# Order of work around the turned gates in a gated-delta-rule layer between two FFNs

## The chip, the core and the metric

The kernel runs on one core of a Trainium2 chip. The time is the device time of one execution in microseconds; the median of three runs of the kernel before is 4090.89 us. Engines work side by side, each through a queue of its own in program order: TensorE (PE), VectorE (DVE), ScalarE (ACT), GpSimd (POOL) and SyncE (SP), which here only issues DMAs. They wait for each other on semaphores.

## The reference

```python
x = x + 0.5 * ffn(layernorm(x))      # spline-built weights
x = x + attn(layernorm(x))
x = x + 0.5 * ffn(layernorm(x))

# attn, for 4 sequences of 512 tokens, 16 key heads of width 128, 2 value heads each
qkvz = x @ W_qkvz                    # q, k, v, z per key head
q, k, v = silu(causal_conv4(q, k, v))
q = rms_norm(q) / D;  k = rms_norm(k) / sqrt(D)
beta = sigmoid(b);    g = -exp(A_log) * softplus(a + dt_bias)
def step(S, q_t, k_t, v_t, g_t, beta_t):       # for every token
    S = S * exp(g_t)
    delta = (v_t - k_t @ S) * beta_t
    S = S + outer(k_t, delta)
    return S, q_t @ S
out = silu(z) * (rms_norm(o) * norm_w)
return out @ W_out
```

## The kernel before

A first FFN runs to about 430 us, the second from about 3790 us. Between them `attn_phase` works through 64 units: a unit is one sequence of 512 tokens of one key head with its two value heads (called head 0 and 1 here), in four chunks of 128 tokens. The recurrence inside a chunk is a triangular system; its 128x128 matrix is inverted in 7 levels of doubling for each head. With the two heads in turn this makes the steps 0 to 13 (`s`; head `s % 2`, level `s // 2`). A step from 2 on is a loop through four engines: TensorE makes a product into the bank `psP` (`at_prod`), VectorE masks it into fp16 (`at_pm`, line 2053), TensorE adds 8 small products into the head's inverse (`psT[g]`, `at_inv`, lines 1675 and 1677), and ScalarE copies that to fp16 (`at_t`, line 1869; `copy_t`). Level 0 (`level_0`, line 1607) seeds the inverse of a head; ScalarE copies it whole (line 1867). Its result for head 0 and 1 of unit j+1 is made at the end of the slot of unit j.

The passes `pe_pass`, `act_pass`, `dve_pass` and `pool_pass` each write out one engine's queue for slots j = -1 to 63. A slot holds the inverse of unit j, its four chunks of recurrence (behind step 15), the preparation of unit j+1 (projections `proj_part`, convolution `tap` and `conv`, `silu`, norms, decays), and the output of unit j-1. The order is written by hand. On TensorE, step s is: product, then the tasks in `fill[s]`, then the inverse products; what is in `fill[s]` hides the mask. `gap[...]` are the tasks between the parts of the chunks. On ScalarE and VectorE the tasks of `steps[s]` stand behind the copy or mask of step s.

The fills are made of these:
- `proj_part(u, first, end)`: products `first` to `end` of 12, 512 columns each, of a projection of unit j+1 (Q, K, V0, V1). `gates_in(u, first, end)`: products of 24, 256 columns each, of Z0 or Z1 of unit j. K, V0 and Z0 share a bank, Q, V1 and Z1 the other; `bank_free` waits for the last reader (for Z0 the last tap of K's convolution).
- `turn_gated(h, j-1)` (line 1528): transposes the gated output of head h of the unit before into the bank `psM` (`at_misc`). It waits for POOL's scaling (`scale_gated`, line 2155) and, for head 1, for VectorE's low half of head 0. ScalarE takes the high half from the bank (`gated`, line 1883, `at_gt_hi`), VectorE the low half (`low`, line 2020, `at_gt_lo`).
- `out_product(c, j-1)`: 6 products with the two halves into the same bank; VectorE adds them to the residual (`out_add`, line 2026) before the next.
- `turn_k`, `turn_kn`, `sums`, `gram_of`, `decay`, `kq_of`: for the norm of k, its product with itself, the decays and q k.

VectorE's `qk(h)` (line 2001) multiplies q k by the decays of head h; its end also releases SP's load of the next weights. At the end of a slot ScalarE squares the outputs (`squares`, line 1877), head 1 first; VectorE multiplies them by the gates of z (line 2094). The output of head 1 lies in `psP`, that of head 0 in `psT[1]`. POOL makes the scales, and in every fourth unit splits the next weights into high and low (lines 2126, 2127), the Z part in two halves, the first when `s_z` tells that Z1's last product is done.

Of the kernel before, what the change touches and what calls it, by code (L numbers as in the profile page):

```python
# [28 lines left out]
ACT = mybir.ActivationFunctionType  # L29
# [5 lines left out]
NK, NV, R = 16, 32, 2  # L35
# [1217 lines left out]
K_U, Q_U, V0_U, V1_U, Z0_U, Z1_U = range(6)  # L1253
# [8 lines left out]
def attn_phase(nc, w_qkvz, conv_w, norm_w, w_out, cst_in, cst16_in, resid, x_hi, x_lo, gate_dram, decay_dram, y_dram):  # L1262
# [7 lines left out]
    with ExitStack() as ctx:  # L1270
# [101 lines left out]
        def wait(eng, name, value):  # L1372

            value += AHEAD.get(name, 0)
            if value > 0:
                eng.wait_ge(sems[name], value)
# [81 lines left out]
        def pe_pass(pe):  # L1458
# [5 lines left out]
            for j, has_delta, has_prep, behind, ends in slots():  # L1464
# [18 lines left out]
                def proj_part(u, first, end, i=j):  # L1483

                    if first == 0:
                        unit = i if u >= Z0_U else i + 1
                        if unit % B == 0:
                            if u >= Z0_U:
                                wait(pe, "p_z", unit // B + 1)
                            else:  # L1490
                                wait(pe, "p_w", 2 * (unit // B) + (1 if u in (K_U, Q_U) else 2))
                        bank_free(u, i)
                    tok = (i if u >= Z0_U else i + 1) % B * S
                    for k in range(first, end):
                        hb = k // 3
                        w, xs = ((w_hi, x_hi), (w_hi, x_lo), (w_lo, x_hi))[k % 3]
                        last = mm(unit_bank[u][:], w[:, hb, UNIT_COL[u]:UNIT_COL[u] + D], xs[:, hb, tok:tok + S], k == 0, k == 3 * HB - 1)
                    if end == 3 * HB:
                        own["s_z" if u >= Z0_U else "s_proj"].up(last)
# [110 lines left out]
                def parts(u, first, end, i=j):  # L1610
                    return lambda: proj_part(u, first, end, i)
# [3 lines left out]
                def gates_in(u, first, end):  # L1615
                    return lambda: gate_part(u, first, end)

                if has_prep:
                    fill[2].append(parts(Q_U, 8, 12))
                if has_delta:  # L1620
                    fill[3].append(gates_in(Z0_U, 0, 6))
                    fill[4].append(gates_in(Z0_U, 6, 16))
                    fill[5].append(gates_in(Z0_U, 16, 20))
                    fill[6].append(gates_in(Z0_U, 20, 24))
                    fill[7].append(gates_in(Z1_U, 0, 10))
                    for s in range(3):
                        fill[9 + s].append(gates_in(Z1_U, 10 + 3 * s, 13 + 3 * s))
                if behind:
                    for h in range(R):
                        fill[5 + h].append(lambda h=h: turn_gated(h, j - 1))  # L1630
                    for c in range(WPROD):
                        fill[8 + c].append(lambda c=c: out_product(c, j - 1))
                if has_delta:
                    fill[12].append(gates_in(Z1_U, 19, 24))
                if has_prep:
                    fill[12].append(turn_k)
                    fill[13].append(parts(V0_U, 0, 3))
                    fill[14].append(parts(V0_U, 3, 6))
                    fill[15] += [parts(V0_U, 6, 9), sums]
                    gap[0].append(parts(V0_U, 9, 12))  # L1640
                    gap[1].append(lambda: gram_of(j + 1))
                    gap[2].append(lambda: decay(0))
                    gap[3].append(parts(V1_U, 0, 4))
                    gap[4] += [lambda: decay(1), parts(V1_U, 4, 5)]
                    gap[5].append(parts(V1_U, 5, 9))
                    gap[6].append(parts(V1_U, 9, 12))
                    gap[10] += [lambda: level_0(j + 1, 0), lambda: kq_of(j + 1)]
                    if j + 2 < UNITS:
                        gap[6].append(parts(K_U, 0, 1, j + 1))
                        gap[7].append(parts(K_U, 1, 5, j + 1))  # L1650
                        gap[8].append(parts(K_U, 5, 7, j + 1))
                        gap[9].append(parts(K_U, 7, 12, j + 1))

                if not has_delta:
                    proj(K_U, range(HB))
                    proj_part(Q_U, 0, 8)
                for s in range(R, STEPS):
                    g, level = s % R, s // R
                    if has_delta:

                        if level == 1:
                            wait(pe, "a_hi", R * j + g + 1)
                            wait(pe, "a_sqo", R * j)
                            wait(pe, "d_gate", R * j)
                        wait(pe, "a_t", STEPS * j + s - R + 1)
                        for c in range(CH):
                            last = mm(ch(psP, c), ch(nlhi[:, g], c), ch(t16[:, g, 0], c))
                        own["s_p"].up(last)
                    for task in fill[s]:
                        task()  # L1670
                    if has_delta:

                        wait(pe, "d_p", PSTEPS * j + s - R + 1)
                        for c in range(CH):
                            nc.tensor.matmul(half_of(ch(psT[g], c), level, 0), ch(t16[:, g, 1], c), half_of(ch(pm[:, g], c), level, 0),  # L1675
                                             start=False, stop=True, skip_group_check=True)
                            last = nc.tensor.matmul(half_of(ch(psT[g], CH + c), level, 1), ch(pm[:, g], c),  # L1677
                                                    half_of(ch(t16[:, g, 1], c), level, 1),
                                                    start=False, stop=True, skip_group_check=True)
                        own["s_t"].up(last)  # L1680
# [83 lines left out]
                        task()  # L1764
                if has_prep:
                    if j + 2 < UNITS:
                        proj_part(Q_U, 0, 8, j + 1)
                    level_0(j + 1, 1)
                if ends:
                    for h in range(R):  # L1770
                        turn_gated(h, j)
# [5 lines left out]
        def act_pass(act):  # L1777
            own = counters("a_")
            A = nc.scalar.activation
            for j, has_delta, has_prep, behind, ends in slots():  # L1780
                nxt = (j + 1) % 2
                kh, gcur, at = j // B, *gates_of(j)

                def conv_out(u):
                    return (cv_k[:], cv_q[:], cv_v[:, nxt, 0, :], cv_v[:, nxt, 1, :])[u]

                def tap(u, j=j):

                    wait(act, "s_proj", 4 * j + u + 1)
                    if u == Q_U and has_delta:  # L1790
                        wait(act, "s_kq", j + 1)
                        wait(act, "p_qg", R * (j + 1))
                    if u == V0_U:
                        wait(act, "s_o", j)
                    own["a_tap"].up(A(conv_out(u), unit_bank[u][:], ACT.Copy, scale=cw[(j + 1) // B % 2][:, u, 3:4]))  # L1795

                def tanh(u):

                    if u == K_U:
                        wait(act, "d_silu", j)  # L1800
                    elif u == Q_U:
                        wait(act, "p_silu", 3 * j)
                    elif has_delta:
                        wait(act, "d_z", 2 * j + u - 1)
                    else:
                        wait(act, "p_silu", 3 * j + u - 1)
                    wait(act, "d_conv", 4 * j + u + 1)
                    own["a_th"].up(A(th[:, u % 2, :], conv_out(u), ACT.Tanh, scale=0.5))

                def tanh_z(u):  # L1810
                    if has_prep:
# [73 lines left out]
                steps = {s: [] for s in range(R, STEPS + 1)}  # L1885
                if has_prep and not has_delta:
                    steps[2].append(lambda: tap(K_U))
                if has_prep:
                    steps[2].append(lambda: tap(Q_U))
                    steps[3].append(lambda: tanh(K_U))  # L1890
                if behind:
                    for h in range(R):
                        steps[5 + h].append(lambda h=h: gated(j - 1, h))
                if has_prep:
                    steps[7].append(lambda: tanh(Q_U))
                if has_delta:
# [52 lines left out]
                        squares(h)  # L1949
                if has_prep:  # L1950
                    copy_t(j + 1, 1)
                    tanh(V1_U)
                if ends:
                    for h in range(R):
                        gated(j, h)
# [2 lines left out]
        def dve_pass(dve):  # L1958
# [8 lines left out]
            for j, has_delta, has_prep, behind, ends in slots():  # L1967
# [61 lines left out]
                if has_prep and has_delta:  # L2029
                    steps[2].append(lambda: conv(K_U, (3,)))  # L2030
                if has_delta:
                    steps[2].append(lambda: qk(0))
                    steps[3].append(lambda: qk(1))
                if has_prep:
                    if not has_delta:
                        steps[3].append(lambda: conv(K_U, (1, 2, 3)))
                if has_prep:
                    steps[3].append(lambda: conv(Q_U, (1,)))
                    steps[4].append(lambda: conv(Q_U, (2, 3)))
                if behind:  # L2040
                    for h in range(R):
                        steps[5 + h].append(lambda h=h: low(h, j - 1))
                    for c in range(WPROD):
                        steps[8 + c].append(lambda c=c: out_add(c, j - 1))
                if has_delta:
# [346 lines left out]
```

How the kernel before makes its waits and increments, by code:

```python
            @block.gpsimd  # L380
            def _(pool):
                nc.gpsimd.memset(f32(st_g[:]), 0.0).then_inc(zeroed, 1)
                nc.gpsimd.memset(f32(st_b[:]), 0.0).then_inc(zeroed, 1)
                pool.dma_start(wts[:, 0:2 * GSUM], gsum_in).then_inc(sums_in, 16)
                pool.dma_start(groups(wts, S_FD, 4 * P), dsum_in.rearrange("p (g n) -> p g n", g=4)).then_inc(sums_in, 16)
                for u in range(UNITS + 4):
                    pool.wait_ge(hi_done, u + 1)
                    nc.gpsimd.tensor_tensor(weights(u, False), quarters(merged[:, u % 2, :]), f32(weights(u, True)), ALU.subtract).then_inc(lo_done, 1)
                pool.wait_ge(lo_done, UNITS + 4)
                pool.wait_ge(sums_in, 32)
# [1 line left out]
            @block.vector  # L392
# [4 lines left out]
                def chain(ins):  # L397
                    count[0] += 1
                    ins.then_inc(link, 1)
                    dve.wait_ge(link, count[0])
# [24 lines left out]
                    V.tensor_scalar(d3, c3, 0.5 * step ** 3, None, ALU.mult)  # L425
                    chain(V.tensor_scalar(d1, c1, 0.5 * step, None, ALU.mult))
                    if reach:
                        chain(V.scalar_tensor_tensor(d1, d3, float(reach), d1, ALU.mult, ALU.add))
                dve.wait_ge(tap_g_in, 32)
                cubics(tap_g, phi_g, d_g, NG, 0)
                dve.wait_ge(zeroed, 1)
# [30 lines left out]
                for u in range(UNITS + 4):  # L463
                    if u == 0:
                        dve.wait_ge(eval_in, 32)
                    if u == UNITS:
```

## Time and profile before

| | |
|---|---|
| median of 3 runs | 4090.89 us (4090.2 to 4093.23) |
| profiled execution | 4097.49 us, its span 4095.7 us |
| mean granted TensorE clock | 0.973 |
| PE busy | 3670.1 us, 90% |
| PE weight loads busy | 3033.4 us, 74% |
| POOL busy | 2327.9 us, 57% |
| DVE busy | 2314.6 us, 57% |
| ACT busy | 2058.3 us, 50% |

The busy time of PE includes the tail of each pipelined matmul, so neighbours overlap: the distance between two starts is what a product costs in a full stream. A row of the timeline has the start, the duration, engine, line, operation, output<-inputs, shapes and count, and in brackets the idle time of the engine ahead of it and the instruction whose end released it. Most of TensorE's products have line 1462, that of a helper.

### The profile page before, as it was taken

How to read it: one execution, taken by the hardware profiler on the slowest of the kernel's cores; microseconds unless marked ns; L12 is line 12 of the kernel's file. 1: busy time of each engine (PE TensorE's matmuls, PEld its weight loads, DVE VectorE, ACT ScalarE, POOL GpSimd, SP SyncE). 2: the span in 40 equal slices, each digit the busy share in tenths (PEclk: the TensorE clock that was granted, in tenths of full speed). 3: DMA queues.
4: the chain of work that ended last, by engine and by line, in shares of the span. 5: the costliest groups of instructions: out<-in, count | busy, mean ns of one | idle time of the engine just before them, and what ended most of it. 6: DMA issues, size and time to landing. Idle time of an engine off the chain costs nothing. (4 is left out here: it accounts for less than half of the span.)

```text
span 4095.7 us, 76858 instructions
## 1 busy us (share of the span) xinstructions
PE 3670.1 (90%) x29348; PEld 3033.4 (74%) x29348; DVE 2314.6 (57%) x4155; ACT 2058.3 (50%) x5168; POOL 2327.9 (57%) x2899
## 2 busy tenths in 40 slices
PE   5995699999999999999999999999999999997798
PEld 4884577777777777777777777777777777776587
DVE  4554455555555555555555555555555555554464
ACT  3442355555555555555555555555555555554233
POOL 2111567676767676666666666666666676763111
PEclk8997899999999999999999999999999999998799
DMA  4332100000000000000000000000000000001421
GB/s 175 81 42 55 54 17 28 17 28 17 28 17 28 17 23 22 23 22 23 22 23 22 23 22 23 22 23 22 23 22 19 21 22 22 22 17 37 171 52 32
DMA packets 142395, 140.46 MB, mean 34 GB/s; under 512 B 84176, under 2 KB 115152, under 8 KB 140880
## 3 DMA queue, kind: packets, MB, share of 16 engines
q1 hardware_dynamic: 136992, 120.16, 10.4%
q0 software_dynamic: 4464, 14.36, 0.9%
q8 instruction: 236, 3.87, 0.4%
q14 instruction: 127, 1.04, 0.1%
q10 hardware_dynamic: 576, 1.03, 0.1%
HBM read 109.11 MB, written 26.21 MB: 33 GB/s over the span
## 5 line engine op out<-in xcount | busy, mean ns | idle before, releaser
L1869 ACT ACTIVATE at_t<-at_inv 128x512 f16<-128x512 f32 x768 | 459.2, 598 | 869.9 <-PE at_inv L1677 869.8
L2053 DVE TENSOR_TENSOR at_pm<-at_prod,at_cst 128x512 f16<-128x512 f32 x768 | 525.8, 685 | 103.4 <-PE at_prod L1462 101.2
L1462 PE MATMUL at_proj<-x_hi,at_w_hi 128*128 128x512 f32 x1024 | 443.9, 434 | 25.9 <-POOL at_w_lo L2127 16.1
L1462 PE MATMUL at_proj<-x_hi,at_w_lo 128*128 128x512 f32 x1024 | 421.8, 412 | 0.0
L1462 PE MATMUL at_proj<-x_lo,at_w_hi 128*128 128x512 f32 x1024 | 417.0, 407 | 0.0
L1675 PEld LDWEIGHTS at_inv<-at_pm,at_t 128*128 128x128 f16 x3072 | 202.7, 98 | 286.4 <-DVE at_pm L2053 206.4
L1675 PE MATMUL at_inv<-at_pm,at_t 128*128 128x64 f16 x3072 | 293.4, 196 | 114.9 <-DVE at_pm L2053 107.4
L1462 PE MATMUL at_prod<-at_t,at_nlhi 128*128 128x128 f16 x3584 | 370.7, 220 | 8.6 <-DVE at_pm L2060 0.9
L2212 POOL TENSOR_TENSOR at_gt_lo<-at_cst,at_gates 128x512 fp32r<-128x512 f32 x256 | 261.6, 1043 | 133.1 <-PE at_misc L1462 133.0
L2026 DVE TENSOR_TENSOR resid<-at_misc,resid 128x512 f32<-128x512 f32 x256 | 177.1, 692 | 278.4 <-PE at_misc L1462 278.4
L1462 PE MATMUL at_proj<-at_w_hi,x_lo 128*128 128x256 f32 x1024 | 319.6, 312 | 0.0
L1462 PE MATMUL at_proj<-at_w_hi,x_hi 128*128 128x256 f32 x1024 | 310.5, 303 | 2.6
L1462 PE MATMUL at_proj<-at_w_lo,x_hi 128*128 128x256 f32 x1024 | 296.4, 290 | 0.0
L1978 DVE SCALAR_TENSOR_TENSOR at_cv_v<-at_proj,at_cw,at_cv_v 128x511 f32<-128x511 f32 (+2 forms) x384 | 287.5, 749 | 15.5 <-ACT at_cv_v L1795 2.0
L1677 PE MATMUL at_inv<-at_t,at_pm 128*128 128x64 f16 x3072 | 286.7, 194 | 0.0
L1462 PEld LDWEIGHTS at_prod<-at_t,at_nlhi 128*128 128x128 f16 x3584 | 236.0, 98 | 34.4 <-issue 33.4
L889 PE MATMUL f_ring<-f_x_hi,ffn_w 128*128 128x512 f32 x640 | 247.8, 402 | 2.9 <-DVE f_x_lo L815 2.9
L1934 ACT ACTIVATE at_t<-at_inv,at_gates 128x128 f32<-128x128 f32 x512 | 160.1, 365 | 175.4 <-PE at_inv L1462 175.4
L1923 ACT ACTIVATE at_t<-at_inv 128x256 f32<-128x256 f32 x256 | 98.5, 385 | 290.9 <-PE at_inv L1734 277.0
L1462 PEld LDWEIGHTS at_proj<-x_hi,at_w_hi 128*128 128x128 f32 x1024 | 195.5, 191 | 54.8 <-issue 21.8
L1462 PE MATMUL at_misc<-at_wo_hi,at_gt_hi 128*128 128x512 f32 x512 | 230.3, 450 | 4.0 <-DVE resid L2026 2.4
L2020 DVE SCALAR_TENSOR_TENSOR at_gt_lo<-at_misc,at_nw,at_gt_hi 128x512 fp32r<-128x512 f32 x128 | 96.2, 751 | 228.2 <-ACT at_gt_hi L1883 228.2
(291 smaller groups left out, 10819.0 us busy)
## 6 DMA issues: line engine op xcount, KB each, us to landing
at_gb<-decays SPq DMA_DIRECT2D x64, 512.0 KB, 3.7
at_e<-w_qkvz SPq DMA_DIRECT2D x32, 512.0 KB, 3.7
ffn_weights<-ffn_w SPq DMA_DIRECT2D x1, 11776.0 KB, 36.5
ffn_w<-ffn_weights POOLq DMA_DIRECT2D x4, 2688.0 KB, 23.8
at_gb<-w_qkvz SPq DMA_DIRECT2D x16, 512.0 KB, 3.7
at_gb<-w_out SPq DMA_DIRECT2D x16, 512.0 KB, 3.5
f_xnext<-x_in SPq DMA_DIRECT2D x4, 1024.0 KB, 5.3
f_xres<-x_res SPq DMA_DIRECT2D x4, 1024.0 KB, 5.1
```

The costliest lines, as they stand in the source:

```text
L889: return nc.tensor.matmul(out, lhsT, rhs, start=start, stop=stop)
L1462: return nc.tensor.matmul(out, lhsT, rhs, start=start, stop=stop)
L1675: nc.tensor.matmul(half_of(ch(psT[g], c), level, 0), ch(t16[:, g, 1], c), half_of(ch(pm[:, g], c), level, 0), start=False, stop=True, skip ...
L1677: last = nc.tensor.matmul(half_of(ch(psT[g], CH + c), level, 1), ch(pm[:, g], c), half_of(ch(t16[:, g, 1], c), level, 1), start=False, sto ...
L1869: own["a_t"].up(A(grown(t16[:, s % R].rearrange("p a t -> p (a t)"), s // R), grown(psT[s % R], s // R), ACT.Copy))
L1923: own["a_v"].up(A(vp, psV, ACT.Copy))
L1934: own["a_d"].up(A(delta[:, h, :], ch(psY, h), ACT.Copy, scale=gcur[:, 2, at + c, h:h + 1]))
L1978: ins = V.scalar_tensor_tensor(out[:, s:S], unit_bank[u][:, 0:S - s], cw[(j + 1) // B % 2][:, u, 3 - s:4 - s], out[:, s:S], ALU.mult, ALU.add)
L2020: own["d_lo"].up(V.scalar_tensor_tensor(gt_lo[:, h, :], out_bank[:], nw[:, 0:1], gt_hi[:, h, :], ALU.mult, ALU.subtract))
L2026: own["d_y"].up(V.tensor_tensor(row, out_bank[:], row, ALU.add))
L2053: own["d_p"].up(V.tensor_tensor(pm[:, g].rearrange("p (c t) -> p c t", c=CH), psP[:].rearrange("p (c t) -> p c t", c=CH), mask.unsqueeze(1 ...
L2212: last = G.tensor_tensor(gm[:, k], incl.unsqueeze(1).to_broadcast([P, CH, P]), new_gates[:, g, at:at + CH, h:h + 1].to_broadcast([P, CH, P ...
```

## The change

Nothing is added or taken out of the computation; instructions change their places in three queues and two waits follow them.

- TensorE: `level_0(j, 1)` moves from the end of slot j-1 to step 2 of slot j, behind step 2's product and the last 3 Q products (before: 4; the ninth moves to the end of the slot before). Behind it stand the first 4 products of Z0, so Z0 starts a step earlier; Z1 is 8, 2, 2, 2, 5, 5 products in steps 7, 9, 10, 11, 12, 13 (before 10, 3, 3, 3, 5 to step 12). V0 starts in step 14 (before 13). The product of step 2 waits for the squares of head 1 only, that of step 3 for both.
- ScalarE: the high halves of heads 0 and 1 stand in steps 4 and 5, ahead of the copies of steps 5 and 6 (before: behind them). The tanh of V1 moves from the slot's end to step 2 of the next, Q's tap and K's tanh each a step later.
- VectorE: both `qk` stand behind the mask of step 3 (before: one in step 2). The Q convolution's taps 1 and 2 stand in step 4 (before: 1 in step 3, 2 and 3 in step 4), tap 3 in step 5 behind the low half of head 0.

```diff
                 if has_prep:
-                    fill[2].append(parts(Q_U, 8, 12))
+                    fill[2].append(parts(Q_U, 9, 12))
                 if has_delta:
-                    fill[3].append(gates_in(Z0_U, 0, 6))
-                    fill[4].append(gates_in(Z0_U, 6, 16))
-                    fill[5].append(gates_in(Z0_U, 16, 20))
-                    fill[6].append(gates_in(Z0_U, 20, 24))
-                    fill[7].append(gates_in(Z1_U, 0, 10))
+                    fill[2] += [lambda: level_0(j, 1), gates_in(Z0_U, 0, 4)]
+                    fill[3].append(gates_in(Z0_U, 4, 10))
+                    fill[4].append(gates_in(Z0_U, 10, 18))
+                    fill[5].append(gates_in(Z0_U, 18, 21))
+                    fill[6].append(gates_in(Z0_U, 21, 24))
+                    fill[7].append(gates_in(Z1_U, 0, 8))
                     for s in range(3):
-                        fill[9 + s].append(gates_in(Z1_U, 10 + 3 * s, 13 + 3 * s))
+                        fill[9 + s].append(gates_in(Z1_U, 8 + 2 * s, 10 + 2 * s))
...
                 if has_delta:
-                    fill[12].append(gates_in(Z1_U, 19, 24))
+                    fill[12].append(gates_in(Z1_U, 14, 19))
+                    fill[13].append(gates_in(Z1_U, 19, 24))
                 if has_prep:
                     fill[12].append(turn_k)
-                    fill[13].append(parts(V0_U, 0, 3))
-                    fill[14].append(parts(V0_U, 3, 6))
-                    fill[15] += [parts(V0_U, 6, 9), sums]
+                    fill[14].append(parts(V0_U, 0, 4))
+                    fill[15] += [parts(V0_U, 4, 9), sums]
...
-                            wait(pe, "a_sqo", R * j)
+                            wait(pe, "a_sqo", R * j - 1 + g)
                             wait(pe, "d_gate", R * j)
...
-                        proj_part(Q_U, 0, 8, j + 1)
-                    level_0(j + 1, 1)
+                        proj_part(Q_U, 0, 9, j + 1)
...
+                if has_delta:
+                    steps[2].append(lambda: tanh(V1_U, j - 1))
                 if has_prep:
-                    steps[2].append(lambda: tap(Q_U))
-                    steps[3].append(lambda: tanh(K_U))
+                    steps[3].append(lambda: tap(Q_U))
+                    steps[4].append(lambda: tanh(K_U))
                 if behind:
                     for h in range(R):
-                        steps[5 + h].append(lambda h=h: gated(j - 1, h))
+                        steps[4 + h].append(lambda h=h: gated(j - 1, h))
...
                     copy_t(j + 1, 1)
-                    tanh(V1_U)
...
                 if has_delta:
-                    steps[2].append(lambda: qk(0))
-                    steps[3].append(lambda: qk(1))
+                    steps[3] += [lambda: qk(0), lambda: qk(1)]
                 if has_prep:
                     if not has_delta:
                         steps[3].append(lambda: conv(K_U, (1, 2, 3)))
+                    steps[4].append(lambda: conv(Q_U, (1, 2)))
+                if behind:
+                    steps[5].append(lambda: low(0, j - 1))
                 if has_prep:
-                    steps[3].append(lambda: conv(Q_U, (1,)))
-                    steps[4].append(lambda: conv(Q_U, (2, 3)))
+                    steps[5].append(lambda: conv(Q_U, (3,)))
                 if behind:
-                    for h in range(R):
-                        steps[5 + h].append(lambda h=h: low(h, j - 1))
+                    steps[6].append(lambda: low(1, j - 1))
```

## Rows read from the trace of the kernel before

**Rows 1.** Busy time by engine in unit 30: length, busy (count), PEclk, DMA, GB/s

```profile
2021.89:2073.62 51.73, 47.62 (x419) 39.69 (x419) 30.27 (x55) 28.14 (x75) 34.57 (x43) 1.00 0.07 21
```

**Rows 2.** TensorE's timeline over the end of slot 29 and slot 30

```profile
2019.37 0.40 PE L1462 MATMUL at_proj<-x_lo,at_w_hi 128*128 128x512 f32 x1
2020.21 0.38 PE L1462 MATMUL at_inv<-at_pm,at_cst 128*128 128x512 f16 x1 [0.45 <-ACT at_aqk L1877]
...
2020.65 0.39 PE L1462 MATMUL at_prod<-at_t,at_nlhi 128*128 128x128 f16 x4
...
2022.76 0.28 PE L1462 MATMUL at_proj<-at_w_hi,x_lo 128*128 128x256 f32 x1
2022.87 0.28 PE L1462 MATMUL at_proj<-at_w_lo,x_hi 128*128 128x256 f32 x1
...
2023.74 0.20 PE L1675 MATMUL at_inv<-at_pm,at_t 128*128 128x64 f16 x1 [0.25 <-DVE at_pm L2053]
...
2026.72 0.60 PE L1528 MATMUL at_misc<-at_cst,at_cv_z 128*128 128x128 f32 x4
2027.76 0.20 PE L1675 MATMUL at_inv<-at_pm,at_t 128*128 128x64 f16 x1 [0.43 <-DVE at_pm L2053]
...
2030.32 0.63 PE L1528 MATMUL at_misc<-at_cst,at_cv_z 128*128 128x128 f32 x4 [1.40 <-DVE at_gt_lo L2020]
...
2033.89 0.20 PE L1675 MATMUL at_inv<-at_pm,at_t 128*128 128x64 f16 x1 [1.20 <-DVE at_pm L2053]
...
2050.53 0.66 PE L1568 MATMUL at_misc<-at_cst,at_kn 128*128 128x128 f32 x4
```

**Rows 3.** ScalarE's timeline in slot 30

```profile
2020.85 1.02 ACT L1867 ACTIVATE at_t<-at_inv 128x1024 f16<-128x1024 f32 x1 [0.73 <-PE at_inv L1607]
...
2024.19 0.60 ACT L1869 ACTIVATE at_t<-at_inv 128x512 f16<-128x512 f32 x1 [0.68 <-PE at_inv L1677]
...
2028.21 0.60 ACT L1869 ACTIVATE at_t<-at_inv 128x512 f16<-128x512 f32 x1 [1.44 <-PE at_inv L1677]
2028.70 0.68 ACT L1883 ACTIVATE at_gt_hi<-at_misc,at_nw 128x512 fp32r<-128x512 f32 x1
...
2049.34 1.14 ACT L1838 ACTIVATE at_kn<-at_misc,at_scale 128x128 f32<-128x128 f32 x4
```

**Rows 4.** VectorE's timeline in slot 30

```profile
2019.11 0.69 DVE L2094 TENSOR_TENSOR at_cv_z<-at_prod,at_cv_z 128x512 f32<-128x512 f32 x1 [0.41 <-ACT at_aqk L1877]
...
2021.14 0.69 DVE L2053 TENSOR_TENSOR at_pm<-at_prod,at_cst 128x512 f16<-128x512 f32 x1 [0.69 <-PE at_prod L1462]
...
2025.58 1.52 DVE L1978 SCALAR_TENSOR_TENSOR at_cv_q<-at_proj,at_cw,at_cv_q 128x510 f32<-128x510 f32 x2
...
2029.42 0.75 DVE L2020 SCALAR_TENSOR_TENSOR at_gt_lo<-at_misc,at_nw,at_gt_hi 128x512 fp32r<-128x512 f32 x1 [1.72 <-ACT at_gt_hi L1883]
...
2033.15 0.68 DVE L2053 TENSOR_TENSOR at_pm<-at_prod,at_cst 128x512 f16<-128x512 f32 x1
...
2038.44 0.69 DVE L2026 TENSOR_TENSOR resid<-at_misc,resid 128x512 f32<-128x512 f32 x1 [1.15 <-PE at_misc L1462]
```

**Rows 5.** POOL's timeline in slot 30, and in slot 31 (from 2096 us)

```profile
2022.83 2.04 POOL L2155 TENSOR_TENSOR at_cv_z<-at_cv_z,at_fr 128x512 f32<-128x512 f32 x2
...
2032.06 1.04 POOL L2126 CAST at_w_hi<-at_e 128x1024 fp32r<-128x1024 f32 x1
...
2096.29 0.61 POOL L2126 CAST at_w_hi<-at_gb 128x512 fp32r<-128x512 f32 x1 [2.58 <-PE at_proj L1462]
...
2098.64 0.23 POOL L2218 TENSOR_SCALAR at_rr<-at_ss 128x4 f32<-128x4 f32 x1 [0.38 <-issue]
```

**Rows 6.** Busy time by engine in a stretch of slot 24, columns as in rows 1

```profile
1719.00:1723.20 4.20, 3.98 (x29) 3.75 (x30) 1.84 (x3) 1.18 (x2) 4.20 (x5) 0.59 0.18 69
```

**Rows 7.** TensorE's timeline in slot 24, the second turned gate

```profile
1719.04 0.99 PE L1528 MATMUL at_misc<-at_cst,at_cv_z 128*128 128x128 f32 x4 [1.39 <-DVE at_gt_lo L2020]
```

**Rows 8.** DMA issues by tile: queue, count, KB each, us to landing

```profile
at_e<-w_qkvz SPq DMA_DIRECT2D x32, 512.0 KB, 3.7
```

More of the change, by code:

```diff
@@ L1655, in pe_pass @@
                     proj(K_U, range(HB))
-                    proj_part(Q_U, 0, 8)
+                    proj_part(Q_U, 0, 9)
                 for s in range(R, STEPS):
@@ L1782, in act_pass, with conv_out @@
                 kh, gcur, at = j // B, *gates_of(j)
-                def conv_out(u):
-                    return (cv_k[:], cv_q[:], cv_v[:, nxt, 0, :], cv_v[:, nxt, 1, :])[u]
+                def conv_out(u, i=j):
+                    return (cv_k[:], cv_q[:], cv_v[:, (i + 1) % 2, 0, :], cv_v[:, (i + 1) % 2, 1, :])[u]
                 def tap(u, j=j):
@@ L1795, in tap, with tanh @@
                     own["a_tap"].up(A(conv_out(u), unit_bank[u][:], ACT.Copy, scale=cw[(j + 1) // B % 2][:, u, 3:4]))
-                def tanh(u):
+                def tanh(u, i=j):
                     if u == K_U:
-                        wait(act, "d_silu", j)
+                        wait(act, "d_silu", i)
                     elif u == Q_U:
-                        wait(act, "p_silu", 3 * j)
-                    elif has_delta:
-                        wait(act, "d_z", 2 * j + u - 1)
-                    else:
-                        wait(act, "p_silu", 3 * j + u - 1)
-                    wait(act, "d_conv", 4 * j + u + 1)
-                    own["a_th"].up(A(th[:, u % 2, :], conv_out(u), ACT.Tanh, scale=0.5))
+                        wait(act, "p_silu", 3 * i)
+                    elif i >= 0:
+                        wait(act, "d_z", 2 * i + u - 1)
+                    else:
+                        wait(act, "p_silu", 3 * i + u - 1)
+                    wait(act, "d_conv", 4 * i + u + 1)
+                    own["a_th"].up(A(th[:, u % 2, :], conv_out(u, i), ACT.Tanh, scale=0.5))
                 def tanh_z(u):
```

## The prediction

> **What bounds the kernel now.** I read the busy times of one unit first [rows 1]: of its 51.73 us TensorE is busy in 47.62, at full clock, POOL, the next, in 34.57. 62 units in a row are within 0.6 us of this length. TensorE's queue sets the time, so only its waits and what it executes matter. What is executed doesn't change here; only the order does.
>
> Then I read TensorE's timeline of one unit (unit 30) for its stalls [rows 2]. The reader sees 0.45 us until the squares on ScalarE are done (2020.21), 0.25 and 0.43 us for a mask (2023.74, 2027.76), 1.40 us in front of the second turned gate (2030.32) and 1.20 us for the mask of step 7 (2033.89). The records' ends overlap the next start, so I count from where the stream could have gone on (last start plus pitch; pitches 0.117 us for a 256-column and 0.235 us for a 512-column product). Then the stalls are: squares 0.60, mask 2 0.10, mask 3 0.41, mask 4 0.27, mask 5 0.60, turned gate 1.56, mask 7 1.36, and six small ones behind step 8, 0.93 together: **5.8 us of 51.7**. Nothing larger than that can be won in a unit.
>
> The two largest have one cause. ScalarE takes the high half of a turned gate only after the inverse copy of the same step (2028.70 behind the copy at 2028.21), VectorE takes the low half from it (2029.42) and TensorE's next transpose into the same bank waits for that low half [rows 2 to 4]. The next mask stands behind the low half in VectorE's queue (2033.15).
>
> **Latencies used**, from rows 2 to 4: first product to its mask 0.45 us (2020.65 to 2021.14 is 0.49; I take a little less, as an estimate); mask start to inverse products 0.74 (2033.15 to 2033.89); first inverse product to ScalarE's copy 0.45 (2023.74 to 2024.19); VectorE's pitch 0.61 for a mask, 0.65 to 0.76 for a convolution tap; a fill of n gate products takes 0.09 + 0.117n behind the 0.20 us of the product ahead of it.
>
> **The change part by part**, on unit 30's clock, where the time at which Q's first products run is the same in both.
>
> *First product of step 2 ahead of level 0.* It no longer waits for the squares of head 0, but for the gate product that reads its bank (VectorE 2019.11 + 0.69) and for the ninth Q product (2019.84). It starts at 19.90, not 20.65. Mask 2 is at 20.4, the last K tap at 21.0 to 21.75. TensorE goes on with three Q products (0.79) and level 0 of head 1 from 20.88 (0.43), which is past the squares' end (20.12) by itself: **the 0.60 us stall is gone**. But now two things come late. The first Z product needs the bank of K, free with the last K tap, so it starts at 21.80 (stall 0.49). And ScalarE copies level 0's result at 21.52 instead of 20.85 [rows 3], 1.02 us long, so the product of step 3 can't start before 22.62. Inverse 2 runs at 22.40, 0.5 us later than now (21.89), with 4 gate products (0.47) more behind it: so far nothing is won.
>
> *Steps 3 and 4.* Product 3 at 22.64, mask 3 at 23.09, inverse 3 at 23.84; the two decay products now stand behind that mask (ends 24.9; they delayed mask 3 before), so mask 4 starts at 24.89 and inverse 4 at 25.64 (now 25.72), with 2 gate products more done. Q's tap is at 24.79 on ScalarE and tanh of K at 26.6; the convolution's first two taps follow mask 4 (25.5, 26.25), mask 5 is at 26.93, inverse 5 at 27.68 (now 27.76).
>
> *SP's queue.* The second decay product also releases the load of the next weights. It ends 0.7 us later (24.97), and 3.7 us to landing [rows 8] is before POOL reads them (2032.06, rows 5): nothing, with some 3 us to spare.
>
> *Turned gates.* The first one runs at 26.53. The POOL scaling it needs has ended by 24.9 [rows 5] (2022.83 + 2.04), so nothing new holds it. ScalarE's high half is at 27.18, straight behind it, not 28.70; the low half at 27.90 (now 29.42); the second turned gate at 28.80 (now 30.32; stall 0.23). Mask 6 stands behind the low half and the last Q tap (28.55 to 29.2): 29.20, and inverse 6 at 29.95 (now 30.83; stall 0.7). The second high half is at 29.46, its low half at 30.18, mask 7 at 30.84, inverse 7 at **31.59, now 33.89**. That is 2.30 us earlier, with 8 of Z1's products behind it where there are 10 now.
>
> *Steps 8 to 11.* The output products use one bank: last product, add on VectorE (2038.44, 0.69), next product. That chain makes a step 2.44 us long now, and with 2 gate products in place of 3 it stays 2.44. So the shorter fill wins nothing, and 5 gate products (0.59 us) are owed at step 12.
>
> *Steps 12 and 13 and behind.* Step 12 has the same work. Step 13 has 5 gate products in place of 3 V0 products; its inverse comes at 43.79, now 46.25 (2.46 earlier), owing 3 V0 products (0.70). One of these fills the 0.28 us that the second residual waits for now; the last Newton product is 1.97 us earlier, and the turning of the scaled k, which now waits for ScalarE's scaling (2049.34 + 1.14, then 2050.53), is 2.10 us earlier, since the scaling moved forward by 2.4. From there to the end of the unit every wait is triggered by TensorE's own products, so I carry 2.10 through. The ninth Q product at the unit's end was counted from the start. The tanh of V1 leaves ScalarE's queue behind level 0's copy and stands behind the next one (23.3): POOL needs it at 24.83, so it costs nothing; were it later than that, POOL would slip by the rest, which its idle time ahead of the k scale hides.
>
> *Every fourth unit.* POOL splits the next Z weights in two halves, the first when Z1's last product is done: 2096.29 in unit 31, followed by the scale of k at 2098.64 [rows 5]. Z1's last product moves from step 12 to step 13, so this start is only 0.76 us earlier. On unit 30's clock the scale's chain starts at 46.15 and takes 1.6; k is scaled at 47.85 to 49.0 and turned at 49.04, not 48.43: these units win 1.5 instead of 2.1.
>
> **Sum.** 47 units x 2.10 + 15 x 1.5 = 121, the first and last unit some 2 more: 123 us. The profiled execution took 4097.5 us (span 4095.7); by it 3974. The median is 4090.9, so **3968 us** (ratio 0.970).
>
> **The clock.** From 1719.0 to 1723.2 the granted clock averages 0.59 [rows 6]: it fell to the lower of its two levels (1.2 GHz) just after the 1.39 us stall and ran the turned gate in 0.99 instead of 0.63 us [rows 7]. Twelve of the 62 units show such a fall and are 0.2 to 0.5 us longer, 4 us in all. Unknown after the change: without the 1.4 us stall it may vanish (-4 us); or the stretch of 27.0 to 30.0, which has 1.6 us of stalls and two groups of transposes in 3 us, may bring it oftener. Taken at 0, as neither end is nearer. The Trainium skill ("TensorE: Matmul & The Clock Gate", Part 4: PE-mode transpose) says that transposes don't count as work for the clock gate in the way products do, which speaks against this change: by it the new stretch is the emptier one and (c) below the likelier, while by the row, in which the longest stall comes just before the fall, the new one is the fuller and the sum gains 4 us.
>
> **Rivals.**
> (a) *The masks take the place of the gate waits.* If the first high half comes later than I walk (its transpose stands behind mask 5's chain of two Q taps), low half, last Q tap and mask 6 pile up in VectorE's queue, which already holds 3.5 us of work between 26.9 and 30.8. Each slip of one 0.7 us instruction delays masks 6 and 7 both; with one slip in each the gain is 2.1 - 1.4 = 0.7 us a unit, 45 us: 4046. With half of that, 4007. For it: VectorE is without a pause in that stretch of my walk. Against: the high half waits for nothing but the transpose.
> (b) *The order doesn't act*: what the turned gates wait for is the scaled gate on POOL. Then about 4089. Against: rows 5, 1.6 us of room.
> (c) *Slower, by the clock.* Falls in every unit. The fall in rows 6 lasts (1 - 0.59) / 0.5 x 4.2 = 3.4 us; with TensorE nearly gapless there, each costs up to half of that, 1.7 us. One a unit gives back up to 105 of 123 us (4073); from 4.2 us at the lower clock in each unit on, the kernel is slower; two falls give 4178. For it: the fall exists now in the same steps. Against: 50 of 62 units don't show it with longer stalls than the new ones.
> (d) *Better than walked*: POOL's fourth units keep pace (-9) and the clock falls vanish (-4): 3955.
>
> **How the numbers follow.** Forecast, within 15 us of 3968, with (d): 0.72. (a): 0.15, more likely the half than the whole. (b): 0.04. (c), partly, between 4010 and 4080: 0.05; wholly, slower: 0.04. The range takes in the forecast, (d) with 10 us for what the latencies may err (0.15 us a unit), and (a) up to its half: 3945 to 4012. A difference under 0.2%, 8 us, can't be told from no change. Faster 0.92, same 0.04, slower 0.04.
>
> **What would show it.** In the profile after: units of 49.6 us, every fourth 50.2; high halves starting within 0.1 us of the turned gates' ends; the second turned gate stalled by 0.2 to 0.4 us instead of 1.4; mask 7's stall under 0.3; a new stall near 0.5 us in front of the first Z product or of step 3's product, released by the K tap or by ScalarE's copy; output steps still 2.44 us. The prediction is wrong if step 3's product waits for over 0.8 us, if mask 6 or 7 start over 0.5 us later than walked, or if the clock stands at 0.5 in more than every third unit.

## The result and the profile after

The changed kernel takes 3975.23 us (median of 4 runs, 3972.5 to 3976.0) against 4090.83 us: ratio 0.9715, interval 0.9698 to 0.9732. The forecast was 3968 us and 0.970. The profiled execution took 3976.0 us, its span is 3974.2.

The stages of after; columns: length, busy (count) of PE, PE weight loads, DVE, ACT, POOL, then PEclk, DMA share, GB/s. The first two are units 30 and 31, the third is the middle of the run.

```profile
1967.79:2017.65 49.86, 47.82 (x421) 39.88 (x419) 30.36 (x54) 28.32 (x75) 34.60 (x42) 1.00 0.07 23
2017.65:2067.88 50.23, 48.00 (x420) 39.91 (x418) 30.37 (x54) 28.48 (x75) 38.39 (x47) 1.00 0.12 34
700.00:3500.00 2800.00, 2682.34 (x23426) 2235.14 (x23426) 1702.19 (x3027) 1588.49 (x4148) 1946.91 (x2383) 1.00 0.07 23
```

Unit 30 is 1.87 us shorter than the 51.73 of [rows 1], with the same work (TensorE busy for 47.8 us, before 47.6): what is gone is waiting. Every fourth unit (unit 31 here) takes 50.2 us.

TensorE's timeline of unit 30 after, answering to [rows 2]. Add 54.73 to a time to have it on the clock of the prediction (both kernels' gate product of head 1 at 2019.11).

```profile
1965.32 0.38 PE L1462 MATMUL at_prod<-at_t,at_nlhi 128*128 128x128 f16 x4
...
1967.21 0.39 PE L1462 MATMUL at_proj<-at_w_hi,x_hi 128*128 128x256 f32 x1 [0.30 <-DVE at_cv_k L1979]
1968.11 0.39 PE L1462 MATMUL at_prod<-at_t,at_nlhi 128*128 128x128 f16 x4
...
1971.08 0.20 PE L1676 MATMUL at_inv<-at_pm,at_t 128*128 128x64 f16 x1 [0.16 <-DVE at_pm L2054]
1971.96 0.60 PE L1528 MATMUL at_misc<-at_cst,at_cv_z 128*128 128x128 f32 x4
1973.26 0.20 PE L1676 MATMUL at_inv<-at_pm,at_t 128*128 128x64 f16 x1 [0.69 <-DVE at_pm L2054]
1974.28 0.63 PE L1528 MATMUL at_misc<-at_cst,at_cv_z 128*128 128x128 f32 x4
1975.44 0.20 PE L1676 MATMUL at_inv<-at_pm,at_t 128*128 128x64 f16 x1 [0.53 <-DVE at_pm L2054]
...
1977.13 0.20 PE L1676 MATMUL at_inv<-at_pm,at_t 128*128 128x64 f16 x1
...
1993.98 0.61 PE L1568 MATMUL at_misc<-at_cst,at_kn 128*128 128x128 f32 x4
```

The second turned gate (1974.28) has no stall that the records count; before it was 1.40 us. Step 7's inverse (1977.13) doesn't wait either; before it was 1.20. Part of the waiting only moved: the inverses of steps 5 and 6 (1973.26, 1975.44) wait 0.69 and 0.53 us for their masks, before 0.43 and nothing. The new waits are the ones forecast: the first Z product for K's last tap (1967.21), and step 3's product (1968.11) for ScalarE's copy:

```profile
1966.95 1.02 ACT L1867 ACTIVATE at_t<-at_inv 128x1024 f16<-128x1024 f32 x1 [1.57 <-PE at_inv L1607]
...
1972.02 0.62 ACT L1808 ACTIVATE at_th<-at_cv_k 128x512 f32<-128x512 f32 x1
1972.66 0.69 ACT L1883 ACTIVATE at_gt_hi<-at_misc,at_nw 128x512 fp32r<-128x512 f32 x1
...
1975.01 0.69 ACT L1883 ACTIVATE at_gt_hi<-at_misc,at_nw 128x512 fp32r<-128x512 f32 x1 [0.70 <-PE at_misc L1528]
```

The copy ends at 1967.97 and the product starts 0.14 us later. Both high halves start within 0.1 us of the end of their transpose (1971.96 + 0.60, 1974.28 + 0.63). For the first it is close: the tanh of K ahead of it in ScalarE's queue ends at 1972.64, so a longer tanh would have held it. VectorE's timeline from mask 4 on, where mask 6 follows a tap and mask 7 a low half without a pause:

```profile
1970.34 0.68 DVE L2054 TENSOR_TENSOR at_pm<-at_prod,at_cst 128x512 f16<-128x512 f32 x1
1970.94 1.53 DVE L1979 SCALAR_TENSOR_TENSOR at_cv_q<-at_proj,at_cw,at_cv_q 128x511 f32<-128x511 f32 x2
1972.51 0.69 DVE L2054 TENSOR_TENSOR at_pm<-at_prod,at_cst 128x512 f16<-128x512 f32 x1
1973.38 0.75 DVE L2021 SCALAR_TENSOR_TENSOR at_gt_lo<-at_misc,at_nw,at_gt_hi 128x512 fp32r<-128x512 f32 x1 [0.18 <-ACT at_gt_hi L1883]
1974.05 0.73 DVE L1979 SCALAR_TENSOR_TENSOR at_cv_q<-at_proj,at_cw,at_cv_q 128x509 f32<-128x509 f32 x1
1974.71 0.68 DVE L2054 TENSOR_TENSOR at_pm<-at_prod,at_cst 128x512 f16<-128x512 f32 x1
1975.73 0.75 DVE L2021 SCALAR_TENSOR_TENSOR at_gt_lo<-at_misc,at_nw,at_gt_hi 128x512 fp32r<-128x512 f32 x1 [0.34 <-ACT at_gt_hi L1883]
1976.39 0.68 DVE L2054 TENSOR_TENSOR at_pm<-at_prod,at_cst 128x512 f16<-128x512 f32 x1
```

### The profile page after: what moved, and what is told of

Read it like the earlier page. It is cut to its first block and busy times, and to the rows that moved or that the text cites. A ratio compares the mean times of both kernels' runs of the same rounds, so it can differ in the third digit from the quotient of the medians.

```text
span 3974.2 us, 76858 instructions
## 1 busy us (share of the span) xinstructions
PE 3665.3 (92%) x29348; PEld 3025.6 (76%) x29348; DVE 2319.6 (58%) x4155; ACT 2069.1 (52%) x5168; POOL 2330.8 (59%) x2899
## 5 line engine op out<-in xcount | busy, mean ns | idle before, releaser
L1462 PE MATMUL at_proj<-at_w_hi,x_lo 128*128 128x256 f32 x1024 | 308.5, 301 | 0.0
L2075 DVE SCALAR_TENSOR_TENSOR at_t<-at_t,at_dcy,at_inv 128x128 f32<-128x128 f32 x256 | 77.5, 344 | 253.2 <-PE at_inv L1462 245.1
```

The source lines that it names most:

```text
L1462: return nc.tensor.matmul(out, lhsT, rhs, start=start, stop=stop)
L2075: ins = V.scalar_tensor_tensor(state[:, h, :], state[:, h, :], dcy[:, h, c:c + 1], ch(psU, h), ALU.mult, ALU.add)
```

## The experiments

Theory A follows the prediction's walk, its account of a unit instruction by instruction: the early high halves carry the gain, and the move of level 0 wins nothing. Its rival, theory B, is that the moves work only together. Each time is a median of 4 runs, each ratio is to the kernel before on the same chip (4093 to 4095 us).

### The high halves alone, and the change without them

`high_only` is the kernel before with one line changed; `no_high` is the changed kernel with that line turned back.

```diff
-                        steps[5 + h].append(lambda h=h: gated(j - 1, h))
+                        steps[4 + h].append(lambda h=h: gated(j - 1, h))
```

> The kernel before with one edit: ScalarE's two high halves stand in steps 4 and 5 instead of 5 and 6. Theory A (the high halves carry the gain; the other moves of the change cost more than they bring): by the same walk, low half at 28.05, second turned gate at 28.9, mask 7 at 30.95, inverse 7 at 31.7 instead of 33.89, with all 10 Z1 products behind it; nothing is given back later, POOL's fourth units keep pace, so 2.1 to 2.2 us a unit: 3955 us, below the changed kernel's 3975. Theory B (the moves work together; without the level-0 move and the later taps the early high half meets a blocked mask): 4000 to 4040. If the fall of the clock hangs on the 1.4 us stall, it is gone here too.

Measured: 3965.82 us, ratio 0.9684 (0.9670 to 0.9699). A unit is 49.73 us, 2.0 shorter, and the fourth units are nearly as short (49.8):

```profile
1964.42:2014.15 49.73, 47.63 (x419) 39.70 (x418) 30.27 (x55) 28.25 (x75) 34.65 (x43) 1.00 0.07 22
```

So one line brings at least as much as the whole change. By the units it brings more (49.73 us against 49.86, a fourth one 49.8 against 50.2), but the intervals of the two ratios overlap a little. Theory B, which had 4000 us or more, is out. The time is 11 us above theory A's 3955; where these went was not followed.

> The changed kernel with only ScalarE's high halves back behind the copies of steps 5 and 6. Theory A: the high half slips to 29.0, the second turned gate to 30.6, inverse 7 to about 34.8, with 8 gate products where before has 10: 2.9 us a unit more than the changed kernel, 4155 us, slower than the kernel before. Theory B: between the two, 4020 to 4080.

Measured: 4243.42 us, ratio 1.0359 (1.0330 to 1.0387), 88 us above theory A's 4155, and slower than the kernel before. A unit in which the clock stays up takes 52.8 us (between 900 and 1270 us every second one is such a unit). That is 1.06 us more than before, and 2.9 more than in the changed kernel, as theory A had it. Nearly all of the rest is the clock. The waits around the turned gates in one unit of this kernel:

```profile
2087.39 0.20 PE L1676 MATMUL at_inv<-at_pm,at_t 128*128 128x64 f16 x1 [0.69 <-DVE at_pm L2054]
2089.94 0.63 PE L1528 MATMUL at_misc<-at_cst,at_cv_z 128*128 128x128 f32 x4 [1.51 <-DVE at_gt_lo L2021]
2091.11 0.20 PE L1676 MATMUL at_inv<-at_pm,at_t 128*128 128x64 f16 x1 [0.54 <-DVE at_pm L2054]
```

Four stretches of it: the steps with these stalls, the steps behind them, the remainder of that unit, and the middle of the run.

```profile
2084.00:2091.50 7.50, 4.60 (x58) 3.75 (x58) 5.27 (x8) 3.33 (x6) 7.34 (x9) 1.00 0.23 72
2091.50:2100.00 8.50, 7.67 (x50) 6.29 (x48) 3.42 (x5) 2.89 (x5) 8.40 (x8) 0.60 0.19 62
2100.00:2145.00 45.00, 42.08 (x363) 35.24 (x361) 26.44 (x49) 25.22 (x69) 25.09 (x34) 1.00 0.04 13
...
700.00:3500.00 2800.00, 2580.31 (x21602) 2151.42 (x21600) 1572.73 (x2792) 1455.55 (x3836) 1789.60 (x2198) 0.95 0.07 21
```

TensorE is busy in 4.60 of 7.50 us, and in the 8.5 us behind them the granted clock averages 0.60. Between 530 and 3540 us the records hold 51 falls of the granted clock to the lower level, 310 us in all; the kernel before holds 10 there (34 us; with one at either end they are the twelve of the prediction), the changed kernel none. A unit with one short fall (3.4 us) is 53.0 to 53.3 us long, one with a long fall (6.8 us) mostly 54.4 to 54.9. From 1327 us on nearly every unit has the long one, 54.6 us from one to the next, at the same place of the unit. The excess of these units over 52.8 us, or 53.1 for a fourth one, adds up to some 80 of the 88 us.

### One high half

`high0_only`: head 0's half in step 4, head 1's left in step 6.

```diff
-                        steps[5 + h].append(lambda h=h: gated(j - 1, h))
+                        steps[4 + 2 * h].append(lambda h=h: gated(j - 1, h))
```

> The kernel before with only head 0's high half early (step 4), head 1's behind the copy of step 6 as before. Theory A: the second turned gate runs at 28.9, but its low half ends at 31.9, so mask 7 at 31.9 and inverse 7 at 32.6 in place of 31.9 with both early: two thirds of the gain, 1.3 us a unit, 4010 us. The 1.4 us stall is gone, the one in front of mask 7 is not; if the falls of the clock need the first, there are none, if any 1.2 us stall will do, there are.

Measured: 4007.32 us, ratio 0.9788 (0.9772 to 0.9805), a unit 50.45 us (-1.28): the first half is worth 1.3 us a unit, the second 0.7. The clock doesn't fall, though the 1.20 us stall for mask 7 stays: in these kernels the falls go with the stall in front of the second turned gate, not with this one.

### The masks' order, with and without the high halves

`high_masks` adds VectorE's new order to `high_only`; `masks_only` has it without the high halves.

```diff
-                    steps[2].append(lambda: qk(0))
-                    steps[3].append(lambda: qk(1))
+                    steps[3] += [lambda: qk(0), lambda: qk(1)]
...
-                    steps[3].append(lambda: conv(Q_U, (1,)))
-                    steps[4].append(lambda: conv(Q_U, (2, 3)))
-                if behind:
-                    for h in range(R):
-                        steps[5 + h].append(lambda h=h: low(h, j - 1))
+                    steps[4].append(lambda: conv(Q_U, (1, 2)))
+                if behind:
+                    steps[5].append(lambda: low(0, j - 1))
+                if has_prep:
+                    steps[5].append(lambda: conv(Q_U, (3,)))
+                if behind:
+                    steps[6].append(lambda: low(1, j - 1))
```

> The kernel before with the early high halves and VectorE's new order (both decay products behind mask 3, two Q taps behind mask 4, the third behind the first low half); level 0, all fills, Q's tap and both tanh stay as before. Theory A: mask 3 at 22.59 instead of 23.00, mask 5 at 26.55, inverse 7 at about 31.4, 2.5 us a unit earlier than before with all products behind it: 3935 us, 0.35 us a unit better than the high halves alone. Theory B (the level-0 move is what makes the order pay): not below 3975.

Measured: 3930.06 us, ratio 0.9597 (0.9583 to 0.9611), a unit 49.13 us. This leaves out the move of level 0, that of the Z and V products, and ScalarE's later tap and tanh, and it is 45 us faster than the whole change.

> The kernel before with only VectorE's new order, the high halves staying behind the copies of steps 5 and 6. By the walk, inverse 5 comes 0.5 us earlier than before, but the high half at 28.24 and the third Q tap in front of mask 6 put mask 6 at 30.3, inverse 6 at 31.05 and inverse 7 at 34.1, 0.2 us later than before: at an unchanged clock 4104 us. So the order that brings 36 us with early high halves costs 13 without them. If the clock falls that the changed kernel without its high halves showed come from the stall in front of the second turned gate plus one in front of mask 6, they come here too, in most units, and the time is 4120 to 4190; if they came from the level-0 move, it is 4104 with some ten falls, as before.

Measured: 4114.57 us, ratio 1.0051 (1.0036 to 1.0066). A unit without a fall is 51.9 us, 0.17 longer than before, and every second one has a fall of 3.4 us (29 falls, about 0.3 us each; 4109.21 us in the profiled execution). The time lies between the two that were expected, and so does the number of falls. The masks' order costs 21 us alone and brings 36 with the early halves. The falls don't need the level-0 move, but they are fewer and shorter here than in `no_high`.

### The move of level 0

`high_masks_level0` adds to `high_masks` the move as the change has it (behind the Q products, the ninth of which goes ahead to the slot before), with the Z and V fills and ScalarE's tap and tanh as before. `level0_first` has level 0 directly behind step 2's product. The edit of `high_masks_level0`:

```diff
-                    fill[2].append(parts(Q_U, 8, 12))
+                    fill[2].append(parts(Q_U, 9, 12))
...
+                    fill[2].append(lambda: level_0(j, 1))
...
-                            wait(pe, "a_sqo", R * j)
+                            wait(pe, "a_sqo", R * j - 1 + g)
...
-                        proj_part(Q_U, 0, 8, j + 1)
-                    level_0(j + 1, 1)
+                        proj_part(Q_U, 0, 9, j + 1)
```

> As the kernel with early high halves and masks, and level 0 of head 1 moved into step 2 with the ninth Q product ahead; the Z, V fills stay as before. Theory A: ScalarE's copy of level 0 holds the product of step 3 to 22.84 instead of 22.14, so inverse 7 comes at about 31.95 with 10 gate products: 0.5 to 0.6 us a unit worse than without the level-0 move, 3970 us, and about equal to the whole change. Theory B: the 0.6 us stall for the squares is won, 3900 to 3925.

Measured: 3975.23 us, ratio 0.9704 (0.9689 to 0.9719), the same median as the changed kernel's, which to the hundredth is chance. A unit is 49.86 us in both. So what the change has beyond this kernel (the Z and V fills, ScalarE's tap and tanh) is worth nothing in a normal unit, and costs 0.3 us in a fourth one (49.9 against 50.2), some 4 us that the two intervals don't tell apart. The move of level 0 costs 45 us. TensorE at step 3 of this kernel:

```profile
1965.89 0.38 PE L1462 MATMUL at_prod<-at_t,at_nlhi 128*128 128x128 f16 x4
...
1968.68 0.38 PE L1462 MATMUL at_prod<-at_t,at_nlhi 128*128 128x128 f16 x4 [0.97 <-ACT at_t L1867]
```

The stall of 0.97 us for ScalarE's copy is what took the place of the 0.45 us for the squares.

`level0_first` against `high_masks_level0`:

```diff
-                    fill[2].append(parts(Q_U, 9, 12))
+                    fill[2] += ([lambda: level_0(j, 1)] if has_delta else []) + [parts(Q_U, 9, 12)]
...
-                    fill[2].append(lambda: level_0(j, 1))
+                    if not has_prep:
+                        fill[2].append(lambda: level_0(j, 1))
```

> Early high halves, masks order, the fills of before (no Z product in step 2), level 0 of head 1 in step 2 directly behind the product and ahead of the Q products. Theory A1: here neither wait is left (copy at 20.9, step 3's product at 22.03, inverse 3 at 23.2 instead of 23.36), so the level-0 move stops costing its 45 us and brings 0.15 us a unit: 3920 us, against 3930 without the move and 3975 with it behind the Q products. Theory C (the move costs by something else, as the queue order of ScalarE): it stays above 3950.

Measured: 3926.38 us, ratio 0.9587 (0.9573 to 0.9602). The cost is gone, so it was the place of the move and not the move itself. ScalarE's copy in it, and TensorE's products of steps 2 and 3 with level 0 between:

```profile
1943.55 1.02 ACT L1868 ACTIVATE at_t<-at_inv 128x1024 f16<-128x1024 f32 x1 [0.80 <-PE at_inv L1607]
```
```profile
1942.69 0.38 PE L1462 MATMUL at_prod<-at_t,at_nlhi 128*128 128x128 f16 x4
1942.91 0.38 PE L1462 MATMUL at_inv<-at_pm,at_cst 128*128 128x512 f16 x1
...
1944.72 0.38 PE L1462 MATMUL at_prod<-at_t,at_nlhi 128*128 128x128 f16 x4 [0.20 <-ACT at_t L1868]
```

Step 3's product is 2.03 us behind step 2's; in the changed kernel 2.79 (1965.32 to 1968.11). It is the three Q products ahead of level 0 that cost, because they delay the 1.02 us copy which step 3 must await. A wait of 0.20 us for the copy is left, where the expectation had none.

`after_level0_first` makes the same swap in the changed kernel, where four Z products also stand in step 2.

```diff
-                    fill[2].append(parts(Q_U, 9, 12))
+                    fill[2] += ([lambda: level_0(j, 1)] if has_delta else []) + [parts(Q_U, 9, 12)]
...
-                    fill[2] += [lambda: level_0(j, 1), gates_in(Z0_U, 0, 4)]
+                    fill[2] += ([] if has_prep else [lambda: level_0(j, 1)]) + [gates_in(Z0_U, 0, 4)]
```

> The changed kernel with level 0 of head 1 directly behind step 2's product, ahead of the three Q products. Theory A1 (two waits of the same length meet at step 3's product: ScalarE's copy and the Z products that need K's last tap): the copy comes 0.8 us earlier, but the Z products still start at 21.94 and inverse 2 at 22.5, so only 0.1 us a unit, 3968 us. Theory A2 (the copy of level 0 alone holds step 3): 0.5 us a unit or more, 3945 us.

Measured: 3973.25 us, ratio 0.9700 (0.9684 to 0.9716), a unit 49.80 us. The copy is 0.8 us earlier, yet the unit only 0.06 shorter, as theory A1 had it. The rows that show why:

```profile
1968.58 0.39 PE L1462 MATMUL at_proj<-at_w_hi,x_hi 128*128 128x256 f32 x1 [0.32 <-DVE at_cv_k L1979]
1969.41 0.38 PE L1462 MATMUL at_prod<-at_t,at_nlhi 128*128 128x128 f16 x4
```

TensorE waits at 1968.58 for K's last tap, and step 3's product stands behind those Z products. In the changed kernel two waits of nearly the same length covered each other; taking one away shows only the other.

### What is left in VectorE's queue

`low1_late` puts the third Q tap behind mask 6 and the second low half behind mask 7, on top of `high_masks`; `level0_first_low1_late` on top of `level0_first`.

```diff
-                    steps[5].append(lambda: conv(Q_U, (3,)))
+                    steps[6].append(lambda: conv(Q_U, (3,)))
...
-                    steps[6].append(lambda: low(1, j - 1))
+                    steps[7].append(lambda: low(1, j - 1))
```

> Early high halves and masks order; VectorE's third Q tap one step later (behind mask 6) and the second low half behind mask 7. Theory A (masks 6 and 7 wait in VectorE's queue behind work that nobody needs yet): inverse 6 at 7.05 instead of 7.70, inverse 7 at 8.75 instead of 9.40, then bound by the ten Z1 products; output product still not held: 0.6 us a unit, 3892 us. Theory D (the second turned gate's chain through ScalarE and VectorE bounds the steps): the output product waits for the low half and gives it back, 3925 us.

Measured: 3902.83 us, ratio 0.9531 (0.9517 to 0.9546): 27 us less than `high_masks`, not 38. Inverse 6 came as forecast (7.03 us behind inverse 2, forecast 7.05). But the Z1 products now wait for the tap, which ends at 1942.20 (0.74 us from 1941.46), and ten of them fill step 7 to its end, so inverse 7 is 8.93 us behind inverse 2 and not 8.75:

```profile
1940.87 0.68 DVE L2054 TENSOR_TENSOR at_pm<-at_prod,at_cst 128x512 f16<-128x512 f32 x1
1941.46 0.74 DVE L1978 SCALAR_TENSOR_TENSOR at_cv_q<-at_proj,at_cw,at_cv_q 128x509 f32<-128x509 f32 x1
1942.27 0.69 DVE L2054 TENSOR_TENSOR at_pm<-at_prod,at_cst 128x512 f16<-128x512 f32 x1
```
```profile
1942.26 0.38 PE L1462 MATMUL at_proj<-at_w_hi,x_hi 128*128 128x256 f32 x1
```

> Both of the two edits above. If they touch different stalls their gains add: 3882 us. If a full TensorE queue bounds first, less.

Measured: 3901.63 us, ratio 0.9528 (0.9514 to 0.9542), where 3882 was expected if the gains add. Against `low1_late` there is no difference that these runs can tell; why the 4 us of `level0_first` don't come back here was not followed. These two are the fastest versions found, some 73 us below the changed kernel.

## Why the prediction was right, point by point

- **The stalls named were the ones that went.** The two in front of the second turned gate and of mask 7 [rows 2] carried the gain, as `high_only` shows: the one line against them brings 2.0 us a unit alone, the whole change 1.87. Against rivals (a) and (b), the rows above show both high halves starting 0.1 us behind their transposes. The argument that the prediction gave for (a) was misread from its own walk, though: VectorE is not without a pause there, the walk leaves 0.4 us ahead of each low half, and the rows have 0.18 and 0.34.
- **Step 2.** "So far nothing is won" held for this place, but understated the price. The Z products started at 21.94 (walk 21.80), the copy at 21.68 (21.52), step 3's product at 22.84 (22.64). Against the order without the move it is a loss of 45 us, which the walk would have shown had it been made for that order too, as the 3970 us expected for `high_masks_level0` show. It was made only against the kernel before.
- **The size of a unit's gain: 1.87 us, not 2.10.** Two latencies were taken too short. The product of step 2 starts at 20.05, 0.25 us behind the end of the gate product it awaits (19.80), where I took 0.10; that alone put the whole walk 0.15 late. The two chained Q taps hold VectorE for 1.57 us up to mask 5, where I took 1.43. Masks 6 and 7 start 0.24 and 0.28 us later than walked, inverse 7 is at 31.86 (walk 31.59), the turned k at 48.71 (walk 48.43). Over the 46 normal units this is some 10 us.
- **Steps 8 to 11 stay 2.44 us** with two products in place of three: they do. VectorE's additions to the residual in unit 30 start at 1979.26, 1981.69, 1984.13 and 1986.57, each 2.43 or 2.44 us behind the last.
- **Every fourth unit wins less**: 50.23 us, walk 50.2. The split in POOL, in unit 31 after:

```profile
2039.22 0.61 POOL L2127 CAST at_w_hi<-at_gb 128x512 fp32r<-128x512 f32 x1 [2.07 <-PE at_proj L1462]
2039.91 1.28 POOL L2128 TENSOR_TENSOR at_w_lo<-at_gb,at_w_hi 128x512 fp32r<-128x512 f32 x1
2041.26 0.23 POOL L2219 TENSOR_SCALAR at_rr<-at_ss 128x4 f32<-128x4 f32 x1
```

  It waits for TensorE's last Z1 product as in [rows 5], and the scale of k follows it without a pause. Where Z1 ends in step 12 as before (`high_only`, `high_masks`), the fourth units are as short as the rest (49.8 and 49.2 us).
- **The clock.** Taken at 0; the falls vanished (PEclk 1.00 above), 4 us better. Rival (c) didn't come in this kernel, but its mechanism is real: `no_high` has it, at some 80 us. The prediction left open whether the stall or the denser transposes would decide; the runs say the stall in front of the second of them. The rule of the Trainium skill on transposes ("TensorE: Matmul & The Clock Gate", Part 4: PE-mode transpose), by which the new stretch should have been the worse, did not show here: the nine kernels without the 1.4 us stall, in which the transposes stand closer together, had no fall in eight cases and a single one in the ninth (`level0_first_low1_late`).
- **The sum.** 46 units of 1.87 and 15 of 1.57 are 110 us, the clock 4, and the two profiled spans differ by 121.5. The last two units gave 8 (from 3679.85 to the last attention product at 3801.95 before, 3566.36 to 3680.58 after) where the sum had some 4; why the last gains more was not followed. So it is partly luck that the forecast of the profiled execution, 3974 us, met the measured 3976: the 10 us that the walk had too much in the normal units were made up by the clock and by the last two units. The medians differ by less, 115.6 us, because the profiled execution of before was 6.7 us above its median and that of after only 0.8.

## What to carry to other kernels

Look first at the place of a consumer in its engine's in-order queue: moving two reads of a bank ahead of copies that were not needed as early took 2 us out of every 51.7, and the rest of the change around them brought nothing more. Walk every part of a combined change against the change without it, not only against the kernel before: a move that only shifts a stall (here level 0, 45 us) hides behind the gain of its neighbour. And where two waits end together, removing one shows next to nothing.

## What was not expected of the hardware

A short stall on TensorE, repeated in a loop, can cost more through the clock than by its own length. With 1.51 us in front of the second transposes and 0.69 and 0.54 us around it, the granted clock fell to its lower level in 51 stretches of `no_high`, and from 1327 us on the falls recurred with the loop, every 54.6 us and 6.8 us long. The order's own price was 1.06 us a unit, the clock's 1.7 in a unit with the long fall. The same stall of 1.40 us gave 10 falls in the kernel before and 29 in `masks_only`; of the nine kernels without it, eight had none and one a single one. What decides between 10, 29 and 51 was not separated.
